# Late steps of a delta-rule recurrence: the largest block of products summed by TensorE through an identity matrix

## The chip, the cores and the metric

The kernel runs on one core of one Trainium2 chip. The metric is the device time of one execution in microseconds (us), here as the median of three runs. A core has TensorE (PE in the profile; its weight loads are PEld), VectorE (DVE), ScalarE (ACT), GpSimd (POOL) and SyncE (SP), which issues most of the DMAs. The engines run beside each other and wait for each other on semaphores.

## The reference

The layer works on 32 sequences of 32 tokens with 512 channels, in float32. It adds three parts to `x`, each after a layer norm: a cross attention to a context of 257 rows, a gated delta rule with 16 heads of 64, and a mixture of 8 experts with top 2 routing. The change lies in the delta rule, whose state is updated token by token:

```
def step(carry, x):
    S_f, S_s = carry
    ...
    S_f = fdt[..., None, None] * S_f
    S_s = sdt[..., None, None] * S_s
    err_f = vt - jnp.einsum('bhk,bhkv->bhv', kt, S_f)
    err_s = vt - jnp.einsum('bhk,bhkv->bhv', kt, S_s)
    bkt = bt[..., None, None] * kt[..., :, None]
    S_f = S_f + bkt * err_f[..., None, :]
    S_s = S_s + bkt * err_s[..., None, :]
    S_fc = _cap(S_f + rf * S_s)
    S_sc = _cap(S_s + rf * S_f)
    ot = fgt[..., None] * jnp.einsum('bhk,bhkv->bhv', qt, S_fc) + sgt[..., None] * jnp.einsum('bhk,bhkv->bhv', qt, S_sc)
```

`_cap` divides a state by max(1, its norm / 64). So each of the 32 steps needs the norm of the states of the step before it.

## The kernel before

The parts follow each other as blocks of code: layer norm, cross attention (`attend`), the projections and Gram matrices of the delta rule (`project`), the recurrence (`recurrence`, line 927), its outputs (`outputs`), routing, and the experts. Each block says what every engine does, in an order written out by hand; a semaphore that an engine waits for is met by a count.

The recurrence never forms the 64 x 64 states. It keeps, for each of the 512 pairs of sequence and head (128 partitions times `SG` = 4), coefficients over the tokens seen so far. `G` holds the Gram matrices of keys, queries and values, `psi` and `phi` are the coefficients of the two states (index `a`), `pr` is `psi` times a column of the key Gram matrix. The costly part of a step is a matrix times vector: for the next token `nxt`, `vp[i] = sum over j of G[i, j] * pr[j]` for the rows i up to `nxt`. There is a matrix of its own for each pair, so VectorE does it in two moves: it makes all the products (`products`, line 1065, into `prod`), and then sums them over j (`sums`, line 1072, a `tensor_reduce`). The matrix is symmetric up to a factor, and only its lower half is used: the rows are cut in blocks of `W` = 8, and the block of rows lo to hi has `min(lo + 8, nxt)` columns. A block has 2 * 4 * (hi - lo) * columns products in each partition, made in two halves (`a` = 0 and 1).

A step `t` on VectorE is written out as one list, with other work between dependent instructions: the reduction of the dots of the last step (line 1079), the products of block 0, `z` (1082), `zz` (1088), the products of the other blocks, the norms (1092, 1095), whose root ScalarE takes (1017), the sums of block 0, the cap (1103, 1106), the sums of the other blocks, the new coefficients `phi` (1114), and then the dots (1119), which read the whole of `vp`, the next `psi` (1041, 1042) and the next `pr` (1046), with which the next step begins. Beside that TensorE computes the gate projection of the layer in the first half of the recurrence (lines 1009, 1010, into all eight banks), ScalarE copies these results out from step 8 on (1021), and GpSimd makes the output weights (990 to 998). The products of a step are overwritten by those of the next.

Of the kernel before, what the change touches and what calls it, by code (L numbers as in the profile page):

```python
# [20 lines left out]
B, N, C = 32, 32, 512  # L21
TOK = B * N
NT = TOK // P
# [10 lines left out]
SG = B * H // P  # L34
BS = P // H
W = 8
# [29 lines left out]
class Chain:  # L66
# [8 lines left out]
    def mark(self, ins):  # L75

        self.n += 1
        ins.then_inc(self.sem, 1)
        return self.n

    def need(self, n):

        self.eng.wait_ge(self.sem, self.base + n)
# [840 lines left out]
                solve(SG - 1, range(N - 1, 0, -1))  # L924


def recurrence(nc, d, ps, xnT, G, gt, phi, wz, rf, gate, wg, wo_in):

    with ExitStack() as ctx:
        sb = lambda name, shape: ctx.enter_context(nc.sbuf_tensor(name, shape, F32))
        sem = lambda name: ctx.enter_context(nc.semaphore(name))
# [3 lines left out]
        prod = sb("r_prod", [P, PROD])  # L937
        z, zz, n2 = sb("r_z", [P, NZ, SG]), sb("r_zz", [P, SG, 3, NZ]), sb("r_n2", [P, 3, SG])
        pr, vp = [sb(f"r_pr{i}", [P, 2, SG, N]) for i in range(2)], sb("r_vp", [P, 2, SG, N])
# [6 lines left out]
        own, zeroed, psi_ready, out_done, stored = sem("r_own2"), sem("r_zeroed"), sem("r_psir"), sem("r_outd"), sem("r_stored")  # L946
        nm_ready, root_ready, blank_out = sem("r_nmr"), sem("r_rootr"), sem("r_blank_out")
        g_in, g_done, g_used, blocks_zero = sem("g_in"), sem("g_done"), sem("g_used"), sem("blocks_zero")
        POOL_STEPS = 4
        LATE = 8  # L950

        def bc(ap, shape):
            return ap.to_broadcast([P] + shape)

        with nc.Block() as block:
            @block.sync
            def _(sp):
                sp.dma_start(wg[:, :, :], d["Wg"].rearrange("(k p) n -> p k n", p=P)).then_inc(g_in, 16)
                for c in range(HC):
# [9 lines left out]
                             d["Wo"].rearrange("(c p) n -> p c n", p=P)).then_inc(wo_in, 16)  # L969
                sp.wait_ge(out_done, N * POOL_STEPS)  # L970
                for s in range(SG):
# [5 lines left out]
            def _(pool):  # L977
# [6 lines left out]
                for t in range(N):  # L984
                    u, m, n = t % PSI, t + 1, t * POOL_STEPS
                    if t == N - 3:
# [13 lines left out]
            @block.tensor  # L1000
            def _(pe):
                pe.wait_ge(g_in, 16 * (HC + 1))
                pe.wait_ge(zeroed, 3)
                for n in range(2 * NT):
                    t, hf = n // 2, n % 2
                    if n >= 8:
                        pe.wait_ge(g_used, n - 7)
                    for k in range(KC):
                        pe.matmul(ps[n % 8], xnT[:, k, t * P:(t + 1) * P], wg[:, k, hf * 512:(hf + 1) * 512], start=(k == 0), stop=False)  # L1009
                    pe.matmul(ps[n % 8], ones[:, :], bg[:, hf * 4:(hf + 1) * 4, :].rearrange("o c p -> o (c p)"),  # L1010
                              start=False, stop=True).then_inc(g_done, 1)

            @block.scalar
            def _(act):
                for t in range(N):
                    act.wait_ge(nm_ready, t + 1)
                    nc.scalar.activation(root[:, :, :], nm[:, :, :], ACT.Sqrt).then_inc(root_ready, 1)  # L1017
                    n = t - LATE
                    if 0 <= n < 2 * NT:
                        act.wait_ge(g_done, n + 1)  # L1020
                        nc.scalar.copy(gate[:, n // 2, (n % 2) * 8:(n % 2 + 1) * 8, :].rearrange("p h k -> p (h k)"), ps[n % 8]).then_inc(g_used, 1)
                act.wait_ge(g_used, 2 * NT)
                for t in range(NT):
                    rows = gate[:, t, :, :].rearrange("p h k -> p (h k)")
                    nc.scalar.activation(rows, rows, ACT.Silu)

            @block.vector
            def _(dve):
# [7 lines left out]
                def spread_states(t):  # L1036

                    u, m = t % PSI, t + 1
                    if t >= PSI:
                        dve.wait_ge(out_done, (t - PSI + 1) * POOL_STEPS)  # L1040
                    stt(psi[u][:, 0, :, 0:m], phi[:, 1, :, 0:m], rf1, phi[:, 0, :, 0:m], ALU.mult, ALU.add)
# [9 lines left out]
                for t in range(N):  # L1051
                    u, m, nxt = t % PSI, t + 1, t + 1
                    rows, parts, at = [], [], 0
                    if nxt < N:
                        need(pr_ready)
                        rows = [(x, min(x + W, nxt + 1), min(x + W, nxt)) for x in range(0, nxt + 1, W)]
                        for lo, hi, cols in rows:
                            size = 2 * SG * (hi - lo) * cols
                            parts.append(prod[:, at:at + size].rearrange("p (a s i j) -> p a s i j", a=2, s=SG, i=hi - lo))
                            at += size  # L1060

                    def products(x, a):
                        if x < len(rows):
                            lo, hi, cols = rows[x]
                            ins = tt(parts[x][:, a], G[:, :, lo:hi, 2, 0:cols], bc(pr[nxt % 2][:, a, :, None, 0:cols], [SG, hi - lo, cols]), ALU.mult)  # L1065
                            return mark(ins)

                    def sums(x):
                        if x < len(rows):
                            lo, hi, cols = rows[x]  # L1070
                            need(made[x])
                            return mark(red(vp[:, :, :, lo:hi].rearrange("p a s i -> p (a s) i"),
                                            parts[x].rearrange("p a s i j -> p (a s) i j"), AX.X, ALU.add))
                        return summed
# [8 lines left out]
                    else:  # L1083
                        products(0, 0)
                    made[0] = products(0, 1)
                    if z_ready is not None:
                        need(z_ready)
# [19 lines left out]
                    if nxt == N:  # L1107
# [7 lines left out]
                    pairs = mark(tt(sc[:, 2:6, :].rearrange("p (a b) s -> p a b s", a=2), bc(sc[:, 0:2, None, :], [2, 2, SG]),  # L1115
                                    bc(sc[:, None, 0:2, :], [2, 2, SG]), ALU.mult))
                    need(summed)
                    for a in range(2):
                        dots_ready = mark(tt(dots[:, a, :, :, 0:nxt], vp[:, :, :, 0:nxt], bc(pr[nxt % 2][:, a, None, :, 0:nxt], [2, SG, nxt]), ALU.mult))
                    need(phi_ready)  # L1120
# [176 lines left out]
def delta_rule(nc, d, ps, ident, x_nat, xnT, w_k, bias, wk_in):  # L1297

    with nc.sbuf_tensor("r_gram", [P, SG, N, 3, N], F32) as G, nc.sbuf_tensor("r_gates", [P, SG, NG + 1, N], F32) as gt, \
            nc.sbuf_tensor("r_phi", [P, 2, SG, N], F32) as phi, nc.sbuf_tensor("r_wz", [P, SG, N, 3, NZ], F32) as wz, \  # L1300
            nc.sbuf_tensor("r_rf", [P, 1], F32) as rf, nc.semaphore("wo_in") as wo_in:
        project(nc, d, ps, ident, xnT, G, gt, phi, wz, rf, w_k, bias, wk_in)
        with nc.sbuf_tensor("o_gate", [P, NT, H, DK], F32) as gate:
            recurrence(nc, d, ps, xnT, G, gt, phi, wz, rf, gate, w_k, wo_in)
            outputs(nc, d, ps, ident, x_nat, gate, w_k[:, :, :].rearrange("p k n -> p (k n)").rearrange("p (c n) -> p c n", c=HC), wo_in,
                    [xnT[:, 2 * s:2 * s + 2, :].rearrange("p k n -> p (k n)").rearrange("p (h n) -> p h n", h=H) for s in range(2)],
                    G[:, :, :, :, :].rearrange("p s i e n -> p (s i e n)"))
# [493 lines left out]
```

## Time and profile before

| | |
|---|---|
| median of 3 runs (lowest, highest) | 1950.63 us (1948.46, 1951.5) |
| the profiled execution | 1954.27 us |
| its span | 1952.5 us |
| VectorE busy over the span | 1192.9 us |
| TensorE busy over the span | 1586.1 us |
| recurrence, from the first row on line 1046 to the last on line 1106 | about 873 to 1126 us |

Busy times are those of an engine's own instructions. PEclk is the clock that TensorE was granted, as a share of 2.4 GHz, so 0.50 is 1.2 GHz. A float32 matmul appears as two matmul records (and two weight loads) in the trace, but a float32 transpose as one. Starts are in microseconds from the start of the span; an instruction's recorded time ends a little after the next one on its engine has begun, because they are pipelined.

### The profile page before, as it was taken

The page shows a single profiled execution, that of the slowest core. Times are in us where ns is not written, and L with a number is a line of the kernel's source. Part 1 is how long each engine was busy: PE and PEld are TensorE (multiplying, and loading weights), DVE is VectorE, ACT ScalarE, POOL GpSimd, SP SyncE. Part 2 cuts the span into 40 slices and gives each one's busy share as a digit, 9 for nine tenths or more (in the row PEclk, how much of TensorE's full clock was granted, in tenths as well). Part 3 has the DMA queues.
Part 4 walks back from the last instruction along what each step waited for, and adds up shares of the span by engine and source line. Part 5 has one row for each costly group of instructions (what it writes and reads, how often), then busy time and mean ns, then how long its engine had stood idle before and what let it go on. Part 6 is the DMA issues. An engine that isn't in the chain of part 4 may idle for free. (4 is left out here: it accounts for less than half of the span.)

```text
span 1952.5 us, 22186 instructions
## 1 busy us (share of the span) xinstructions
PE 1586.1 (81%) x7269; PEld 1151.5 (59%) x7269; DVE 1192.9 (61%) x2594; ACT 711.7 (36%) x1361; POOL 94.9 (5%) x261
## 2 busy tenths in 40 slices
PE   7999999999899999508700059749999999999998
PEld 3777777777677777403200048646666666666664
DVE  4355455465413677999999936344565555555555
ACT  2333333333244545400000032124555555555552
POOL 0000000000000000002111200030000000000003
PEclk9999999999899999858955559769999999999999
DMA  3211010010025145414100042064335515144104
GB/s 114 78 33 32 16 33 24 25 33 16 0 90 91 54 38 91 84 27 153 43 0 0 0 113 65 1 250 174 135 125 177 195 38 199 67 155 173 38 17 135
DMA packets 116457, 153.06 MB, mean 78 GB/s; under 512 B 47217, under 2 KB 68209, under 8 KB 116369
## 3 DMA queue, kind: packets, MB, share of 16 engines
q1 hardware_dynamic: 110640, 137.81, 23.7%
q0 software_dynamic: 2560, 8.39, 1.3%
q10 hardware_dynamic: 3168, 5.77, 0.8%
q8 instruction: 45, 0.74, 0.2%
q14 instruction: 44, 0.35, 0.1%
HBM read 250.32 MB, written 31.39 MB: 144 GB/s over the span
## 5 line engine op out<-in xcount | busy, mean ns | idle before, releaser
L1686 DVE TENSOR_TENSOR gl<-w_gu,gh 128x2048 fp32r<-128x2048 f32 x138 | 290.8, 2107 | 16.5 <-ACT gh L1621 16.5
L1621 ACT CAST gh<-w_gu 128x2048 fp32r<-128x2048 f32 x138 | 242.2, 1755 | 62.3 <-DMA w_gu<-in_up_proj 52.3
L1576 PE MATMUL bank<-w_d,hT 128*128 128x512 f32 x506 | 245.2, 603 | 13.6 <-ACT hT L1645 13.5
L1553 PE MATMUL bank<-gh,xh 128*128 128x512 f32 (+1 forms) x552 | 219.0, 397 | 10.9 <-DVE xl L1677 9.5
L1719 DVE TENSOR_TENSOR hid<-silu,bank 128x256 f32<-128x256 f32 x138 | 55.1, 399 | 262.9 <-ACT silu L1634 262.9
L1555 PE MATMUL bank<-gh,xl 128*128 128x512 f32 (+1 forms) x552 | 206.8, 375 | 0.0
L1554 PE MATMUL bank<-gl,xh 128*128 128x512 f32 (+1 forms) x552 | 206.6, 374 | 0.0
L1182 PE MATMUL bank<-o_v,xnT 128*128 128x64 f32 x256 | 36.1, 310 | 176.0 <-DMA o_v<-scratch_v_rows 176.0
L1576 PEld LDWEIGHTS bank<-w_d,hT 128*128 128x128 f32 x506 | 92.0, 189 | 88.4 <-issue 56.0
L1182 PEld LDWEIGHTS bank<-o_v,xnT 128*128 128x128 f32 x256 | 35.8, 227 | 176.8 <-DMA o_v<-scratch_v_rows 176.8
L1634 ACT ACTIVATE silu<-bank 128x256 f32<-128x256 f32 x138 | 50.7, 367 | 211.6 <-PE bank L1555 211.4
L550 DVE COPY probT<-bank 128x512 f32<-128x512 f32 x64 | 41.2, 683 | 138.5 <-PE bank L434 138.5
L1553 PEld LDWEIGHTS bank<-gh,xh 128*128 128x128 f32 x552 | 104.9, 190 | 32.3 <-DVE xl L1677 9.6
L1009 PE MATMUL bank<-w_kg,xnT 128*128 128x512 f32 x128 | 61.9, 629 | 75.1 <-DMA bg_row<-in_bg 75.1
L1555 PEld LDWEIGHTS bank<-gh,xl 128*128 128x128 f32 x552 | 104.6, 189 | 19.5
L1554 PEld LDWEIGHTS bank<-gl,xh 128*128 128x128 f32 x552 | 105.2, 191 | 14.7
L1017 ACT ACTIVATE r_root<-r_nm 128x8 f32<-128x8 f32 x32 | 6.7, 208 | 274.5 <-DVE r_nm L1095 274.5
L502 ACT ACTIVATE prob<-bank,neg_max 128x257 f32<-128x257 f32 x128 | 59.1, 474 | 86.9 <-DVE neg_max L537 86.9
L1009 PEld LDWEIGHTS bank<-w_kg,xnT 128*128 128x128 f32 x128 | 24.1, 198 | 111.3 <-DMA bg_row<-in_bg 75.3
L489 ACT COPY xv<-bank 128x512 f32<-128x512 f32 x64 | 37.6, 588 | 127.1 <-PE bank L387 127.1
L1065 DVE TENSOR_TENSOR r_prod<-r_gram,r_pr 128x512 f32<-128x512 f32 (+23 forms) x158 | 83.8, 549 | 0.0
L385 PE MATMUL bank<-xa_wkv_hi,ctx_hi 128*128 128x512 f32 x192 | 78.9, 411 | 0.6 <-PEq L280 0.6
(295 smaller groups left out, 3126.0 us busy)
## 6 DMA issues: line engine op xcount, KB each, us to landing
w_gu<-in_gate_proj SPq DMA_DIRECT2D x46, 1024.0 KB
w_gu<-in_up_proj SPq DMA_DIRECT2D x46, 1024.0 KB
w_d<-in_down_proj SPq DMA_DIRECT2D x46, 1024.0 KB
w_gu<-in_gate_proj SPq DMA_DIRECT2D x23, 768.0 KB
w_gu<-in_up_proj SPq DMA_DIRECT2D x23, 768.0 KB
w_d<-in_down_proj SPq DMA_DIRECT2D x23, 768.0 KB
ctx_raw<-in_ctxT SPq DMA_DIRECT2D x32, 385.5 KB, 3.9
scratch_gram<-gram SPq DMA_DIRECT2D x8, 768.0 KB, 3.3
```

What stands on the lines that cost most here:

```text
L385: pe.matmul(bank, hi(k), other_hi(k), start=(k == 0), stop=False)
L502: nc.scalar.activation(prob[s][:, c, :], ps[c][:, 0:M], ACT.Exp, bias=neg_max[s][:, c:c + 1], accum_out=total[s][:, c:c + 1]).then_inc(exp ...
L1009: pe.matmul(ps[n % 8], xnT[:, k, t * P:(t + 1) * P], wg[:, k, hf * 512:(hf + 1) * 512], start=(k == 0), stop=False)
L1065: ins = tt(parts[x][:, a], G[:, :, lo:hi, 2, 0:cols], bc(pr[nxt % 2][:, a, :, None, 0:cols], [SG, hi - lo, cols]), ALU.mult)
L1182: mm = pe.matmul(ps[O_BANK + 2 * s + h // 8][:, (h % 8) * DK:(h % 8 + 1) * DK], outw[s][:, h, :], v_row[s][:, h, :], start=True, stop=True)
L1553: pe.matmul(bank, xh[s % 2][:, k, :], hi, start=(k == 0), stop=False)
L1554: pe.matmul(bank, xh[s % 2][:, k, :], lo, start=False, stop=False)
L1555: mm = pe.matmul(bank, xl[s % 2][:, k, :], hi, start=False, stop=(k == KC - 1))
L1576: mm = pe.matmul(bank, hT[n % 2][:, c, :], w_d[:, b * (BLK // P) + c, :], start=(b == 0 and c == 0), stop=(b == NB - 1 and c == cs[-1]))
L1621: nc.scalar.copy(gh[n % RING][:, :, :, 0:bw].rearrange("p k a f -> p (k a) f"), w_gu[:, :, :, b * BLK:b * BLK + bw].rearrange("p k a f -> ...
L1686: nc.vector.tensor_tensor(gl[n % RING][:, :, :, 0:bw].rearrange("p k a f -> p (k a) f"), w_gu[:, :, :, b * BLK:b * BLK + bw].rearrange("p ...
L1719: nc.vector.tensor_tensor(hid[n % 2][:, 0:bw], silu[n % 2][:, 0:bw], ps[GU_BANK + n % 3][:, bw:2 * bw], ALU.mult).then_inc(hid_done, 1)
```

## The change

From `nxt` = `FIRST_SUM` = 18 on, that is in 14 of the 31 steps that have a matrix times vector, the block with the most products is taken first, and the others follow in their old order. Its products are made by VectorE as before. TensorE then sums them: for each column j it multiplies the 128 x 128 identity matrix (as the stationary operand) with the column's products, all `2 * SG * (hi - lo)` of them (64, or 56 in two steps), and adds up in bank 0. The columns' products lie `cols` elements apart. ScalarE copies the sums from the bank into `vp`, and VectorE waits for that copy ahead of the dots. The reduction of this block on VectorE is left out. The block has 16 columns for `nxt` = 18 to 21, 22 for 22, 23 for 23, 24 for 24 to 29, 30 for 30 and 31 for 31, so there are 314 such matmuls.

```
+        made_for_pe, pe_summed, vp_taken = sem("made_for_pe"), sem("pe_summed"), sem("vp_taken")
+        FIRST_SUM = 18
+        def row_blocks(nxt):
+            blocks = [(x, min(x + W, nxt + 1), min(x + W, nxt)) for x in range(0, nxt + 1, W)]
+            if nxt >= FIRST_SUM:
+                blocks.sort(key=lambda r: -(r[1] - r[0]) * r[2])
+                blocks[1:] = sorted(blocks[1:])
+            return blocks
...
@@ TensorE, behind the gate projection
+                pe.wait_ge(g_used, NT + 1)
+                for nxt in range(FIRST_SUM, N):
+                    k = nxt - FIRST_SUM
+                    lo, hi, cols = row_blocks(nxt)[0]
+                    width = 2 * SG * (hi - lo)
+                    part = prod[:, 0:width * cols].rearrange("p (x j) -> p x j", j=cols)
+                    pe.wait_ge(made_for_pe, 2 * (k + 1))
+                    if k:
+                        pe.wait_ge(vp_taken, k)
+                    for j in range(cols):
+                        mm = pe.matmul(ps[0][:, 0:width], ident[:, :], part[:, :, j], start=(j == 0), stop=(j == cols - 1))
+                    mm.then_inc(pe_summed, 1)
...
@@ ScalarE, step t, behind the root and the gate's copy
+                    k = t + 1 - FIRST_SUM
+                    if 0 <= k < N - FIRST_SUM:
+                        lo, hi, cols = row_blocks(t + 1)[0]
+                        act.wait_ge(pe_summed, k + 1)
+                        nc.scalar.copy(vp[:, :, :, lo:hi], ps[0][:, 0:2 * SG * (hi - lo)].rearrange("p (a s i) -> p a s i", a=2, s=SG)
+                                       ).then_inc(vp_taken, 1)
...
@@ VectorE, step t
-                        rows = [(x, min(x + W, nxt + 1), min(x + W, nxt)) for x in range(0, nxt + 1, W)]
+                        rows = row_blocks(nxt)
...
                             ins = tt(parts[x][:, a], G[:, :, lo:hi, 2, 0:cols], bc(pr[nxt % 2][:, a, :, None, 0:cols], [SG, hi - lo, cols]), ALU.mult)
+                            if x == 0 and nxt >= FIRST_SUM:
+                                ins.then_inc(made_for_pe, 1)
+                                return None
                             return mark(ins)
...
                     def sums(x):
-                        if x < len(rows):
+                        if x < len(rows) and not (x == 0 and nxt >= FIRST_SUM):
...
                     need(summed)
+                    if nxt >= FIRST_SUM:
+                        dve.wait_ge(vp_taken, nxt - FIRST_SUM + 1)
                     for a in range(2):
                         dots_ready = mark(tt(dots[:, a, :, :, 0:nxt], vp[:, :, :, 0:nxt], bc(pr[nxt % 2][:, a, None, :, 0:nxt], [2, SG, nxt]), ALU.mult))
```

VectorE, the step with `nxt` = 26, from the dots' reduction to the dots, as it stands before (`r_zr` is what comes of the dots, `r_prod` the products, `r_vp` their sums, and the last number is the elements in each partition):

```order
L1079 TENSOR_REDUCE r_zr<-r_dots 128x16
L1065 TENSOR_TENSOR r_prod<-r_gram,r_pr 128x256
L1082 TENSOR_TENSOR r_z<-r_zr,r_sc 128x16
L1065 TENSOR_TENSOR r_prod<-r_gram,r_pr 128x256
L1088 TENSOR_TENSOR r_zz<-r_wz,r_z 128x120
...
L1072 TENSOR_REDUCE r_vp<-r_prod 128x8x8
L1103 TENSOR_SCALAR r_root<-r_root 128x8
L1072 TENSOR_REDUCE r_vp<-r_prod 128x8x8
L1106 RECIPROCAL r_cap<-r_root 128x8
L1072 TENSOR_REDUCE r_vp<-r_prod 128x8x8
L1111 TENSOR_TENSOR r_sc<-r_cap,r_gates 128x8
L1072 TENSOR_REDUCE r_vp<-r_prod 128x8x3
```

And the same places of the same step in the change (line 1094 is the products, 1104 the sums):

```order
L1111 TENSOR_REDUCE r_zr<-r_dots 128x16
L1094 TENSOR_TENSOR r_prod<-r_gram,r_pr 128x768
L1114 TENSOR_TENSOR r_z<-r_zr,r_sc 128x16
L1094 TENSOR_TENSOR r_prod<-r_gram,r_pr 128x768
L1120 TENSOR_TENSOR r_zz<-r_wz,r_z 128x120
...
L1135 TENSOR_SCALAR r_root<-r_root 128x8
L1104 TENSOR_REDUCE r_vp<-r_prod 128x8x8
L1138 RECIPROCAL r_cap<-r_root 128x8
L1104 TENSOR_REDUCE r_vp<-r_prod 128x8x8
L1143 TENSOR_TENSOR r_sc<-r_cap,r_gates 128x8
L1104 TENSOR_REDUCE r_vp<-r_prod 128x8x3
```

The pair of products at the head of the step grew from 256 to 768 elements each, the pair of 768 later in the step is gone in exchange, and of four reductions three are left.

TensorE, behind the last gate matmul; the blocks for `nxt` = 18 to 21, then 22, 23 to 29, 30 and 31:

```order
L1021 MATMUL bank<-bg_row,ones_row 128x512
L1033 MATMUL bank<-r_prod,ident 128x64 x64
L1033 MATMUL bank<-r_prod,ident 128x56 x22
L1033 MATMUL bank<-r_prod,ident 128x64 x167
L1033 MATMUL bank<-r_prod,ident 128x56 x30
L1033 MATMUL bank<-r_prod,ident 128x64 x31
```

These 314 matmuls are new; before, TensorE had nothing here until the outputs.

## Rows read from the trace of the kernel before

**Rows 1.** The page, busy time of each engine over the span
```profile
PE 1586.1 (81%) x7269; PEld 1151.5 (59%) x7269; DVE 1192.9 (61%) x2594; ACT 711.7 (36%) x1361; POOL 94.9 (5%) x261
```
**Rows 2.** Windows: stretch, its length; busy us and instructions of PE, PEld, DVE, ACT, POOL; clock; DMA
```profile
1050.00:1070.00 20.00, 0.00 (x0) 0.00 (x0) 19.93 (x51) 0.21 (x1) 3.00 (x7) 0.50 0.00 0
```
**Rows 3.** Timeline of VectorE, the step with nxt = 26: start, time, instruction
```profile
1042.12 0.57 DVE L1079 TENSOR_REDUCE r_zr<-r_dots 128x16 f32<-128x400 f32 x1
1042.60 0.41 DVE L1065 TENSOR_TENSOR r_prod<-r_gram,r_pr 128x256 f32<-128x256 f32 x1
1043.02 0.42 DVE L1065 TENSOR_TENSOR r_prod<-r_gram,r_pr 128x256 f32<-128x256 f32 x1
...
1049.53 1.70 DVE L1072 TENSOR_REDUCE r_vp<-r_prod 128x64 f32<-128x1536 f32 x1
...
1052.55 0.65 DVE L1119 TENSOR_TENSOR r_dots<-r_vp,r_pr 128x208 f32<-128x208 f32 x2
...
1053.83 0.52 DVE L1046 TENSOR_TENSOR r_pr<-r_psi,r_gram 128x216 f32<-128x216 f32 x1
1054.38 0.59 DVE L1079 TENSOR_REDUCE r_zr<-r_dots 128x16 f32<-128x416 f32 x1
```
**Rows 4.** Groups of VectorE by shape, 955 to 1130 us: busy us, mean ns
```profile
L1065 DVE TENSOR_TENSOR r_prod<-r_gram,r_pr 128x512 f32<-128x512 f32 x30 | 20.5, 684 | 0.0
L1072 DVE TENSOR_REDUCE r_vp<-r_prod 128x64 f32<-128x1024 f32 x15 | 18.2, 1213 | 0.0
L1065 DVE TENSOR_TENSOR r_prod<-r_gram,r_pr 128x768 f32<-128x768 f32 x16 | 14.6, 952 | 0.0
L1072 DVE TENSOR_REDUCE r_vp<-r_prod 128x64 f32<-128x1536 f32 x8 | 13.6, 1701 | 0.0
...
L1065 DVE TENSOR_TENSOR r_prod<-r_gram,r_pr 128x992 f32<-128x992 f32 x2 | 2.3, 1183 | 0.0
...
L1072 DVE TENSOR_REDUCE r_vp<-r_prod 128x64 f32<-128x1984 f32 x1 | 2.2, 2209 | 0.0
```
**Rows 5.** Timeline of VectorE, starts of the first (nxt = 18) and behind the last step (31)
```profile
963.11 0.44 DVE L1079 TENSOR_REDUCE r_zr<-r_dots 128x16 f32<-128x272 f32 x1
...
969.55 0.67 DVE L1119 TENSOR_TENSOR r_dots<-r_vp,r_pr 128x144 f32<-128x144 f32 x2
...
971.34 0.45 DVE L1079 TENSOR_REDUCE r_zr<-r_dots 128x16 f32<-128x288 f32 x1
...
1123.27 0.66 DVE L1079 TENSOR_REDUCE r_zr<-r_dots 128x16 f32<-128x496 f32 x1
```
**Rows 6.** Timeline of the outputs behind the recurrence: matmuls, and ScalarE behind them
```profile
1140.46 7.09 PE L1182 MATMUL bank<-o_v,xnT 128*128 128x64 f32 x32 [175.98 <-DMA o_v<-scratch_v_rows]
...
1147.67 1.08 ACT L1225 ACTIVATE r_gram<-bank 128x512 f32<-128x512 f32 x2 [9.22 <-PE bank L1182]
...
1152.89 1.97 PE L1192 MATMUL bank<-ident,r_gram 128*128 128x128 f32 x8 [5.34 <-DVE r_gram L1289]
...
1154.65 6.92 PE L1182 MATMUL bank<-o_v,xnT 128*128 128x64 f32 x32
1161.34 0.77 PE L1206 MATMUL bank<-wo_hi,o_gT_hi 128*128 128x512 f32 x1
...
1169.64 3.68 PE L1182 MATMUL bank<-o_v,xnT 128*128 128x64 f32 x32
```
**Rows 7.** Windows, columns as in rows 2: behind the gate's matmuls, and in the outputs
```profile
964.00:966.00 2.00, 0.48 (x2) 0.00 (x0) 2.00 (x7) 0.00 (x0) 0.00 (x0) 1.00 0.03 4
966.00:968.00 2.00, 0.00 (x0) 0.00 (x0) 2.00 (x6) 0.68 (x2) 0.00 (x0) 0.85 0.88 274
...
1158.00:1160.00 2.00, 2.00 (x11) 2.00 (x11) 0.00 (x0) 0.00 (x0) 0.00 (x0) 0.50 0.00 0
1164.00:1166.00 2.00, 2.00 (x7) 1.58 (x6) 1.97 (x4) 0.31 (x1) 0.00 (x0) 0.66 0.90 235
```
**Rows 8.** Groups by shape: ScalarE's smallest copy out of a bank over 128 partitions
```profile
L293 ACT COPY k_last<-bank 128x128 f32<-128x128 f32 x1 | 0.3, 266 | 29.1 <-PE bank L312 29.1
```

More of the change, by code:

```diff
@@ L924, in _, with recurrence @@
                 solve(SG - 1, range(N - 1, 0, -1))
-def recurrence(nc, d, ps, xnT, G, gt, phi, wz, rf, gate, wg, wo_in):
+def recurrence(nc, d, ps, ident, xnT, G, gt, phi, wz, rf, gate, wg, wo_in):
     with ExitStack() as ctx:
@@ L1303, in delta_rule @@
         with nc.sbuf_tensor("o_gate", [P, NT, H, DK], F32) as gate:
-            recurrence(nc, d, ps, xnT, G, gt, phi, wz, rf, gate, w_k, wo_in)
+            recurrence(nc, d, ps, ident, xnT, G, gt, phi, wz, rf, gate, w_k, wo_in)
             outputs(nc, d, ps, ident, x_nat, gate, w_k[:, :, :].rearrange("p k n -> p (k n)").rearrange("p (c n) -> p c n", c=HC), wo_in,
```

## The prediction

> **What bounds the kernel now.** I read the page first, then windows of 20 us over the recurrence, then VectorE's timeline of single steps, and last the rows of TensorE that are nearest to the new matmuls. The page gives shares over the whole span and says little here: TensorE is the busier engine [rows 1], but not in the recurrence. In the window over its late steps VectorE is busy 19.93 of 20 us, while TensorE does nothing and its clock stands at 0.50, and ScalarE has 0.2 us of work [rows 2]. So in this stretch each microsecond that leaves VectorE's list is a microsecond gained, and each one that VectorE waits is one lost. The question is whether TensorE is done when VectorE comes to the dots.
>
> **What leaves VectorE.** The reductions taken away are that of 1024 elements four times (1.21 us each), that of 1536 six times (1.70), and one each of about 1.4, 1.6, 1.9 and 2.21 us; the first three of those four lie between the rows shown, in proportion to size [rows 4]. That is 4.9 + 10.2 + 7.1 = 22.2 us. Products are neither added nor removed. That their order changes costs nothing: what stood between dependent instructions was the products of a small block and is now that of a large one, so each gap is covered as before. The root is asked for before some 2.4 us of products, so ScalarE has it ready although the first reduction no longer stands ahead of line 1103. If nothing waited, the kernel would be 22 us faster.
>
> **What TensorE needs for one column.** The nearest rows are the head mixes of the outputs (line 1182): the same float32 form, 64 moving columns and a 128 x 128 stationary operand. 32 records, which are 16 matmuls, take 7.09 us from the first start to the last end, at a clock of 0.50 [rows 6]. One record lasts about 0.47 us, so their starts are (7.09 - 0.47) / 31 = 0.214 us apart, and a matmul of two records costs 0.427 us. At full clock the same 32 take 3.68 us, which makes 0.22 us a matmul. The transposes at the low clock, with 128 moving columns, are also (1.97 - 0.47) / 7 = 0.214 us apart [rows 6]. So what paces both is not the number of moving columns but the load of the weights, and the 56 columns of two steps will gain nothing. The identity is the same for every column, yet each matmul loads it: the page counts as many loads as matmuls [rows 1], although other places of the kernel use a stationary operand twice in a row.
>
> **Which clock.** 1.2 GHz, for these reasons. From 1152.89 to 1161.34 TensorE runs transposes and then such mixes for 8.4 us without a pause, and the window at 1158 to 1160 shows 0.50 still; so do the 7.09 us before. Only after the wide matmuls of 512 columns begin at 1161.34 does the clock rise, within the window 1164 to 1166 (mean 0.66) [rows 6, 7]. The new bursts look like the mixes, last 7 to 13 us, and stand apart by the rest of a step, some 4 us. A rule of the Trainium skill speaks the other way (TensorE: Matmul & The Clock Gate, Part 1 on the two states): sustained activity of TensorE releases the full clock, and idle time takes it back. The trace holds it for the wide matmuls and contradicts it for these narrow ones; what it would give here is a rival below. Only the first burst begins warm. The last gate matmul ends at 964.5, and the clock falls about 967.4 (mean 0.85 over 966 to 968) [rows 7]. With the first burst beginning at about 964.9, some 2.5 us of it run at double rate: -2.5 us.
>
> **The stride.** The 64 elements of a column are 64 to 124 bytes apart. No matmul of the trace reads so. VectorE does: line 1046 takes a strided column of the Gram matrix and needs 0.52 us for 216 elements, where line 1119 needs about 0.36 for each of its two instructions of 208 with neighbours side by side [rows 3]. Less 0.15 us that the smallest instructions take, that is 1.7 ns against 1.0 an element, a factor of 1.7. On TensorE 64 columns at 1.2 GHz are 53 ns, with this factor 90 ns, and 0.214 us pass in any case for the load. So I take nothing for the stride. The two bounds: nothing, and, if loads and streams did not overlap at all and the stride doubled the stream, 0.214 + 0.107 = 0.32 us a record, 0.64 us a matmul. I take the lower, since the equal spacing at 64 and 128 columns shows a stream hidden behind its load. The Trainium skill states against this change (SBUF — State Buffer, the note on cachelines) that float32 reads which touch a new 16-byte line each time pay a penalty; it gives no price, and by the rule alone the sum would lie anywhere up to the rival on the stride.
>
> **One step.** Take `nxt` = 26 [rows 3]. It lasts 1054.38 - 1042.12 = 12.26 us. In the change TensorE may start when both large products are done: the reduction on line 1079 (0.48 us to the next start), then twice 0.95 us [rows 4], 2.4 us after the step's start. Then come 24 x 0.427 = 10.25 us, and around them 0.69 us: the tail of the last record 0.26, VectorE to TensorE 0.06 and TensorE to ScalarE 0.12 (1147.55 to 1147.67) [rows 6], ScalarE's copy 0.22 (0.27 for 128 elements) [rows 8], and 0.03 to VectorE. Then VectorE has left what it does from the dots to the next step, 1.83 us. The path through TensorE is 2.4 + 10.25 + 0.69 + 1.83 = 15.2 us, VectorE's own list 12.26 - 1.70 + 0.08 = 10.6. So TensorE decides, and the step becomes 2.9 us longer, not 1.6 shorter; VectorE waits 4.6 us ahead of the dots. Queued behind that wait are psi, z and pr, so the whole next step; GpSimd and ScalarE only follow.
>
> **The sum.** The same in all steps: the first has 1.7 + 16 x 0.427 + 0.69 + 1.79 = 11.0 us in place of 8.23 [rows 5], and the TensorE path wins there too, by 4 us (the smallest lead, at `nxt` = 21, is 2.5 us). So the 14 steps can be added up as one path. From 963.11 to 1123.27 they take 160.2 us now [rows 5]. In the change: 314 matmuls x 0.427 = 134.1; the head's two products, 24.7 (4 x 1.37 + 6 x 1.90, and 7.8 in the other four, up to 2 x 1.18) [rows 4]; the reduction ahead of them 14 x 0.47 = 6.6; 14 x 0.69 = 9.7; from dots to the next step 24.7 (1.79 at first, 1.83 in the middle, 14 of them). That is 199.8 us, 39.6 more than now; with the warm start 37.1. What comes after is only shifted: the output's DMAs start when GpSimd is done, and the transfer of Wo hangs on the gate's matmuls alone. The profiled execution has 1952.5 us of span and 1.8 around it, 1954.3; the change would make it 1991.4. The median of the runs is 3.6 lower, so I forecast **1988 us**.
>
> **The rivals.**
> *The clock is full throughout* (1932 us, 5%). At 0.222 us a matmul the 24 columns take 5.3 us, with 0.65 around them, and VectorE has 6.3 us of other work there in the step above. Then VectorE's list decides in nearly all late steps, and 18.4 us of the 22.2 are gained. For it: the first burst starts warm. Against it: the clock falls within 3 us of an idle TensorE [rows 7], and a warm burst would leave about 4 us idle in each step.
> *The clock rises within each burst* (1952 us, 7%). This is what the skill's rule on the clock would make of it, and I price it by rows: as with the wide matmuls, 4.0 us at the low clock [rows 6, 7], the rest at the high one. The 24 columns then need 7.2 us in place of 10.25, the steps come out between 0.6 us shorter and 1 us longer than now, and the sum is +1.5 us. The 8.4 us at 0.50 speak against it.
> *The stride or the lack of overlap sets the pace* (2020 to 2055 us, 14%): 0.53 to 0.64 us a matmul instead of 0.427, which is 314 x (0.10 to 0.21) = 32 to 67 us on top of the forecast. For it: no row shows such a read on TensorE.
> *It does not do what it says*, say the reductions stay: excluded, since three of the four stand in the list of VectorE and 314 matmuls in that of TensorE.
>
> The point from which the sign turns is the price of a matmul: at 0.30 us the sum is nil, and each 0.01 us is worth 3 us. The forecast's 0.427 is well above it, the full clock's 0.22 below.
>
> **How the numbers follow.** The forecast has 72%; its own range is 1981 to 2000, from 0.41 to 0.46 us a matmul and 0.15 us either way in the 0.69. The strided rival has 14%, the clock within a burst 7%, the full clock 5%, others 2%. To hold 8 in 10 the range takes in the forecast and the lower part of the strided rival, and reaches down for a clock that is high part of the time: 1974 to 2040 us. A difference under 0.2%, or 3.9 us, cannot be told from none in this kernel. Faster: 6% (the full clock, and a little of the third case). Same: 6%. Slower: 88%.
>
> **What would show it.** In the profile of the changed kernel: 628 records on the new matmul's line, 0.214 us apart, at a clock of 0.50; in the timeline of VectorE an idle time ahead of the dots of 2.5 to 6 us in each of the 14 steps, 60 us in all, released by ScalarE's copy; a step with `nxt` = 26 of 15.2 us; a first burst shorter than the next three. The forecast is wrong if the window over the late steps shows a clock near 1.00, if starts are more than 0.22 us apart at the low clock (the stride), or if VectorE's idle time is small.

## The result

The changed kernel takes 1987.33 us (median of 4 runs, 1985.96 to 1988.35), the kernel before 1950.46 us beside it. The ratio is 1.018, with an interval of 1.017 to 1.020. The forecast was 1988 us.

The page after, busy time of each engine over the span; it answers to [rows 1]:

```profile
span 1985.0 us, 23470 instructions
...
PE 1720.2 (87%) x7897; PEld 1285.0 (65%) x7897; DVE 1172.5 (59%) x2580; ACT 714.8 (36%) x1375; POOL 95.3 (5%) x261
```

There are 628 records more on TensorE, two for each of the 314 matmuls, and VectorE has 20.4 us less to do. TensorE has 134.1 us more. The sum had 134.1 for its matmuls, but that the two agree to the tenth is chance: the new bursts shown below add up to 135.4 us, and the sum leads to 134.1 less 2.5 for the warm start plus 14 tails of 0.26, 135.2.

The timeline of VectorE over the first and behind the last of the 14 steps, to be held against [rows 5]:

```profile
964.61 0.44 DVE L1111 TENSOR_REDUCE r_zr<-r_dots 128x16 f32<-128x272 f32 x1
...
1161.30 0.66 DVE L1111 TENSOR_REDUCE r_zr<-r_dots 128x16 f32<-128x496 f32 x1
```

The stretch of the 14 steps grew from 160.16 to 196.69 us. These 36.5 us are the whole difference (1987.33 - 1950.46 = 36.9). Below, "the stretch" always means this one, from the first of these reductions to the last.

The step with `nxt` = 26, all engines, to be held against [rows 3]:

```profile
1064.05 0.57 DVE L1111 TENSOR_REDUCE r_zr<-r_dots 128x16 f32<-128x400 f32 x1
1064.53 0.95 DVE L1094 TENSOR_TENSOR r_prod<-r_gram,r_pr 128x768 f32<-128x768 f32 x1
...
1065.48 0.95 DVE L1094 TENSOR_TENSOR r_prod<-r_gram,r_pr 128x768 f32<-128x768 f32 x1
...
1077.05 0.21 ACT L1049 COPY r_vp<-bank 128x64 f32<-128x64 f32 x1 [9.15 <-PE bank L1033]
1077.36 0.66 DVE L1153 TENSOR_TENSOR r_dots<-r_vp,r_pr 128x208 f32<-128x208 f32 x2 [4.67 <-ACT r_vp L1049]
...
1079.20 0.59 DVE L1111 TENSOR_REDUCE r_zr<-r_dots 128x16 f32<-128x416 f32 x1
```

It lasts 15.15 us in place of 12.26. The bracket on the dots is VectorE's idle time, 4.67 us, ended by ScalarE's copy. Over the stretch, the view of who waited for whom (sum, times, longest):

```profile
DVE r_dots L1153 <- ACT r_vp L1049: 56.9, 14, 5.7
```

And TensorE's bursts, the first two, that of `nxt` = 26 and the last:

```profile
966.47 4.73 PE L1033 MATMUL bank<-r_prod,ident 128*128 128x64 f32 x32 [0.40 <-DVE r_prod L1094]
974.88 7.09 PE L1033 MATMUL bank<-r_prod,ident 128*128 128x64 f32 x32 [3.67 <-DVE r_prod L1094]
...
1066.49 10.52 PE L1033 MATMUL bank<-r_prod,ident 128*128 128x64 f32 x48 [4.60 <-DVE r_prod L1094]
...
1146.05 13.49 PE L1033 MATMUL bank<-r_prod,ident 128*128 128x64 f32 x62 [5.33 <-DVE r_prod L1094]
```

The 32 records of 16 columns take 7.09 us, exactly as long as the mixes of [rows 6]. The windows over the first burst and within the one of `nxt` = 26 and the last (columns as in rows 2):

```profile
966.00:968.00 2.00, 1.60 (x15) 1.56 (x14) 2.00 (x8) 0.42 (x2) 0.00 (x0) 1.00 0.24 56
968.00:970.00 2.00, 2.00 (x17) 2.00 (x15) 1.96 (x8) 0.26 (x1) 0.86 (x3) 0.76 0.90 282
...
1066.00:1076.00 10.00, 9.51 (x45) 9.51 (x45) 6.70 (x18) 0.21 (x1) 1.66 (x4) 0.50 0.00 0
1146.00:1159.00 13.00, 12.96 (x61) 12.96 (x61) 8.15 (x17) 0.21 (x1) 1.78 (x4) 0.50 0.00 1
```

TensorE is never idle for 13 us and the clock stays at 0.50. In the first burst it even falls, about 969, while the narrow matmuls run. That is 3 us after the last wide matmul of the gate, which ended at 966.1. In the kernel before the clock fell 2.9 us after it (964.5 to 967.4), with TensorE idle in between. As far as the clock shows, the narrow matmuls made no difference to it.

### The profile page after: what moved, and what is told of

Its sections match the earlier page's. It is cut to its first block and busy times, and to the rows that moved or that the text cites. A ratio compares the mean times of both kernels' runs of the same rounds, so it can differ in the third digit from the quotient of the medians.

```text
span 1985.0 us, 23470 instructions
## 1 busy us (share of the span) xinstructions
PE 1720.2 (87%) x7897; PEld 1285.0 (65%) x7897; DVE 1172.5 (59%) x2580; ACT 714.8 (36%) x1375; POOL 95.3 (5%) x261
## 5 line engine op out<-in xcount | busy, mean ns | idle before, releaser
L1720 DVE TENSOR_TENSOR gl<-w_gu,gh 128x2048 fp32r<-128x2048 f32 x138 | 290.8, 2108 | 16.3 <-ACT gh L1655 16.3
L1033 PE MATMUL bank<-r_prod,ident 128*128 128x64 f32 (+1 forms) x628 | 135.4, 404 | 58.1 <-DVE r_prod L1094 58.1
L1033 PEld LDWEIGHTS bank<-r_prod,ident 128*128 128x128 f32 x628 | 132.7, 327 | 61.4 <-DVE r_prod L1094 60.2
L1094 DVE TENSOR_TENSOR r_prod<-r_gram,r_pr 128x256 f32<-128x256 f32 (+21 forms) x158 | 83.8, 549 | 0.0
L1597 PEld LDWEIGHTS bank<-ident,hid 128*128 128x128 f32 x253 | 35.3, 140 | 67.3 <-issue 49.5
```

Of the source, the lines that this page charges most:

```text
L1033: mm = pe.matmul(ps[0][:, 0:width], ident[:, :], part[:, :, j], start=(j == 0), stop=(j == cols - 1))
L1597: mm = pe.transpose(ps[H_BANK + n % 2][:, c * P:(c + 1) * P], hid[n % 2][:, c * P:(c + 1) * P], ident[:, :])
L1720: nc.vector.tensor_tensor(gl[n % RING][:, :, :, 0:bw].rearrange("p k a f -> p (k a) f"), w_gu[:, :, :, b * BLK:b * BLK + bw].rearrange("p ...
```

## The experiments

The theory: TensorE's time for the block, paced by records of 0.214 us at the low clock, lies between the products and the dots, and VectorE waits for it. The rivals are VectorE's own list in its new order, contention, a fixed cost of the hand-over, the stride, and the clock.

**Order alone.** The new order of the blocks, with all sums left on VectorE:

```
-                        rows = [(x, min(x + W, nxt + 1), min(x + W, nxt)) for x in range(0, nxt + 1, W)]
+                        rows = row_blocks(nxt)
```

> The kernel before with the blocks in the new order (largest first from nxt = 18 on), all of them still summed by VectorE, no matmuls and no copies. Theory (the order costs nothing, each gap between dependent instructions is covered as before): 1950.5 us, within 0.2% of before. Rival (part of the loss is VectorE's own list in the new order): up to 0.5 us a step, 1957 us.

Measured: 1952.50 us against 1951.78, ratio 1.0005 (0.9996 to 1.0015). The stretch is 160.23 us, 0.07 longer than before. The order costs nothing.

**TensorE beside VectorE, and nobody late.**

```
-                    for j in range(cols):
+                    for j in range(cols // 2):
...
-                        nc.scalar.copy(vp[:, :, :, lo:hi], ps[0]
+                        nc.scalar.copy(aside[:, :, :, lo:hi], ps[0]
...
-                        if x < len(rows) and not (x == 0 and nxt >= FIRST_SUM):
+                        if x < len(rows):
```

> The changed kernel, but VectorE sums every block itself as before, and TensorE sums half of the largest block's columns (8 to 15) into the bank; ScalarE copies this half sum into a tile that nobody reads; VectorE keeps its wait for the copy ahead of the dots. Theory (the whole loss is the wait, and TensorE at work beside VectorE costs VectorE nothing): TensorE needs 8 x 0.427 + 0.69 = 4.1 us to 15 x 0.427 + 0.69 = 7.1 us and VectorE has 4.8 to 10 us of work there, so the copy is always in time: 1950.5 us within 0.2%, no idle time of VectorE ahead of the dots. Rival (contention for the memory, or the semaphores and the copy, cost something in themselves): 0.3 us or more a step, 1955 us or more.

Measured: 1953.62 us, ratio 1.0013 (1.0004 to 1.0023). The stretch is 160.27 us, and the trace has no wait ahead of the dots. So half the matmuls, all the copies and all the semaphores of the change cost 0.1 us where VectorE does not wait for them. The median is 1.8 us longer, but the profiled execution, 1951.88 us, is not one of the longer ones, so its trace cannot say where these 1.8 us lie; their cause stays open. Half of the columns is also half of the time beside VectorE. For the full bursts the changed kernel's own rows speak: the products of 256 elements that run beside a burst take 0.42 us there and 0.41 or 0.42 before. The loss of the change is the wait.

**Neighbours side by side.**

```
-                        mm = pe.matmul(ps[0][:, 0:width], ident[:, :], part[:, :, j], ...)
+                        mm = pe.matmul(ps[0][:, 0:width], ident[:, :], prod[:, j * width:(j + 1) * width], ...)
```

> The changed kernel, but each matmul reads 64 (56) neighbouring elements of the products instead of a column with its elements 64 to 124 bytes apart. Other products are added up than the computation asks for; number, size and order of the instructions are the same. Theory (the weight load paces the matmuls): starts stay 0.214 us apart, 7.09 us for the 32 records of 16 columns, time 1987 us within 3. Rival (the stride costs something): records closer together and a time below 1980 us, in proportion.

Measured: 1982.59 us in one run. Its burst of `nxt` = 26:

```profile
1064.78 10.51 PE L1033 MATMUL bank<-r_prod,ident 128*128 128x64 f32 x48 [4.59 <-DVE r_prod L1094]
```

10.51 us against 10.52: at the low clock the stride costs nothing. The stretch is 196.6 us, the changed kernel's 196.7. The 4 to 5 us by which this single run is shorter do not come from there, so I read the trace and not the total.

**Half the width.**

```
+                        mm = pe.matmul(ps[0][:, 0:width // 2], ident[:, :], part[:, 0:width // 2, j], ...)
```

> The changed kernel, but each matmul takes only half of the rows of the block (32 or 28 moving columns in place of 64 or 56); the sums of the other half are left out. Theory (the load of the 128 x 128 stationary operand paces): nothing changes, 0.214 us from record to record, 1987 us within 3. Rival (TensorE's time goes with the elements it sums): the wait ahead of the dots falls by 3.4 to 6.6 us a step, some 60 us of TensorE time less, and the time comes down to 1935 us or less.

Measured: 1986.13 us in one run.

```profile
1065.61 10.45 PE L1033 MATMUL bank<-r_prod,ident 128*128 128x32 f32 x48 [4.60 <-DVE r_prod L1094]
```

With 32 moving columns in place of 64 the same 48 records take 10.45 us. What is paid for is not the summed elements but the records, each with its load of the identity. That it is the load, and not some other fixed price of a record, no run separates. The loads of the kernel before, with 4, 16, 32, 80 and 128 stationary columns, all in stretches at full clock but for a few records, speak for it:

```profile
L430 PEld LDWEIGHTS bank<-ident,prob 128*4 128x4 f32 x32 | 2.7, 86 | 0.4
L706 PEld LDWEIGHTS bank<-q_sq,head_cols 128*16 128x16 f32 x64 | 3.9, 94 | 10.4 <-issue 9.4
L308 PEld LDWEIGHTS bank<-xa_wkv,ctx_last 128*32 128x32 f32 x6 | 0.6, 109 | 2.0 <-issue 2.0
L723 PEld LDWEIGHTS bank<-xnT,w_gates 128*80 128x80 f32 x32 | 4.5, 149 | 3.3 <-issue 1.7
L303 PEld LDWEIGHTS bank<-xnT,xa_wq 128*128 128x128 f32 x64 | 12.1, 190 | 16.0 <-issue 15.7 <-DVE qT L321 0.2
```

From 16 to 128 columns a load grows by 96 ns, 0.86 ns a column. For 128 columns that is 0.11 us, an estimate from these rows, and the narrow records of the first, warm burst start 0.11 us apart.

**One record a column.**

```
+        prod_r = ctx.enter_context(nc.sbuf_tensor("r_prod_r", [P, 2 * SG * W * (N - 1)], F32R))
+        ident_r = ctx.enter_context(nc.sbuf_tensor("r_ident_r", [P, P], F32R))
...
-                        mm = pe.matmul(ps[0][:, 0:width], ident[:, :], part[:, :, j], ...)
+                        mm = pe.matmul(ps[0][:, 0:width], ident_r[:, :], part[:, :, j], ...)
```

> The changed kernel, but the products of the largest block and the identity are kept as fp32r, so that a column is one matmul record (and one weight load) and not two; the products are rounded to fp32r. Theory (records of 0.214 us at a clock of 0.50 pace TensorE): a column costs 0.214 us, 24 columns 5.1 us, which is less than VectorE's other work from nxt = 25 on, and the kernel comes out like the rival of the full clock, 1932 us, between 1929 and 1937. Rival (a fixed cost of the hand-over from VectorE to TensorE to ScalarE and back makes a good part of the loss): the waits fall by less than half, 1955 us or more.

Measured: 1934.58 us, ratio 0.991 (0.989 to 0.993). The burst of `nxt` = 26, and the waits for the copy over the stretch:

```profile
1041.18 5.33 PE L1037 MATMUL bank<-r_prod_r,r_ident_r 128*128 128x64 f32 x24 [4.77 <-DVE r_prod_r L1102]
```

```profile
DVE r_dots L1161 <- ACT r_vp L1054: 0.7, 2, 0.4
```

24 records instead of 48, half the time, still at 0.50 of the clock, and the wait is gone: 0.7 us in all. The stretch is 139.95 us. The same change of the kernel loses 1.8% with two records a column and gains 0.9% with one. The fixed part of the hand-over does not make the loss: it is the same here, and the wait is gone.

**A warm TensorE.** Wide matmuls behind each burst:

```
+                    for _ in range(5):
+                        pe.matmul(ps[1], ident[:, :], G[:, 0, :, :, :].rearrange("p i e n -> p (i e n)")[:, 0:512], start=True, stop=True)
```

> The changed kernel with five wide matmuls (512 moving columns of the Gram matrix, into a bank that nobody reads) behind each burst of narrow ones, so that TensorE is busy while VectorE makes the next products. Theory (wide matmuls raise the clock after about 4 us, narrow ones do not hold it): from the second or third step on a burst begins at a clock of 1.00 and falls to 0.50 some 2.5 us later, as the first burst of the changed kernel did; the 24 columns take about 8 us in place of 10.5, and the time is 1960 us, between 1952 and 1970. Rivals: the clock, once high, is held through the burst, 1935 us; or it never rises, and the wide matmuls, which last 4.3 us at the low clock, only push the early bursts back, 1988 us or more.

Measured: 1971.03 us in one run, just past the end of what I gave. TensorE's timeline in the third step and in that of `nxt` = 24 (line 1034 the narrow ones, 1039 the wide), and then windows over the latter:

```profile
985.45 3.71 PE L1034 MATMUL bank<-r_prod,ident 128*128 128x64 f32 x32
988.99 4.49 PE L1039 MATMUL bank<-r_gram,ident 128*128 128x512 f32 x10
...
1027.08 9.06 PE L1034 MATMUL bank<-r_prod,ident 128*128 128x64 f32 x48
1035.95 7.04 PE L1039 MATMUL bank<-r_gram,ident 128*128 128x512 f32 x10
```

```profile
1027.00:1029.00 2.00, 2.00 (x14) 1.92 (x13) 2.00 (x8) 0.68 (x2) 0.00 (x0) 1.00 0.00 0
1029.00:1031.00 2.00, 2.00 (x14) 2.00 (x14) 2.00 (x5) 0.00 (x0) 1.10 (x3) 0.96 0.00 0
1031.00:1033.00 2.00, 2.00 (x12) 2.00 (x11) 0.79 (x4) 0.00 (x0) 0.44 (x1) 0.50 0.00 0
...
1037.00:1039.00 2.00, 2.00 (x4) 0.89 (x3) 1.97 (x9) 0.00 (x0) 0.00 (x0) 0.50 0.00 0
1039.00:1041.00 2.00, 2.00 (x3) 0.67 (x2) 2.00 (x5) 0.00 (x0) 0.00 (x0) 0.50 0.02 4
1041.00:1043.00 2.00, 2.00 (x7) 0.93 (x6) 2.00 (x7) 0.21 (x1) 0.00 (x0) 0.98 0.00 0
```

The clock rises and falls much as expected, and the time is neither rival's. In the steps with 16 columns a burst is over in 3.7 us, at full clock. The burst of `nxt` = 30 keeps it too, for 6.8 us. In the other long ones the clock falls while they run, in the step shown about 4 us after the narrow matmuls begin (at 1031), though TensorE is never idle, and comes back about 5 us after the wide ones begin (at 1041). The wide ones then last 7.04 us at the low clock and hold back the next burst, which is one reason why it came out 11 us above the 1960.

The other reason is in the same trace. At full clock the narrow records are not 0.11 us apart in every step. Here are a window within the burst of `nxt` = 25, with 24 columns, and the burst of `nxt` = 30, with 30, and a window within it:

```profile
1043.00:1047.00 4.00, 4.00 (x27) 4.00 (x27) 3.65 (x11) 0.00 (x0) 1.67 (x4) 1.00 0.03 6
```

```profile
1115.92 6.83 PE L1034 MATMUL bank<-r_prod,ident 128*128 128x56 f32 x60
```

```profile
1116.00:1122.00 6.00, 6.00 (x56) 6.00 (x55) 6.00 (x14) 0.21 (x1) 1.24 (x3) 1.00 0.00 0
```

The starts of single records are 0.160 us apart with 24 columns, and 0.111 with 16 or 30. The elements of a column lie 96 bytes apart with 24 columns, 64 with 16 and 120 with 30. So the distance may well cost something at the full clock that the 0.214 us of the low clock cover. No run has neighbours side by side in such a burst at full clock, so this is not shown. The bursts of 24 columns took 8.6 to 9.1 us and not the 8 that I had expected. Worked out from these rows, the step with `nxt` = 26 would last 12.6 us at full clock throughout (2.4 + 24 x 0.32 + 0.65 + 1.83), no less than the 12.26 before. That is an estimate. The clock is worth much here, but in these steps it would not have turned the sign, and wide matmuls that compute nothing are a poor way to it.

**Four columns a matmul.** Four partial sums a row stay in the bank, and VectorE sums them itself in place of ScalarE's copy:

```
+                        for j in range(0, cols, PER):
+                            some = min(PER, cols - j)
+                            mm = pe.matmul(bank[:, :, lo - low:hi - low, 0:some], ident[:, :], part[:, :, :, j:j + some], ...)
...
+                        dve.wait_ge(pe_summed, nxt - FIRST_SUM + 1)
+                        red(vp[:, :, :, low:high].rearrange("p a s i -> p (a s) i"),
+                            ps[0][:, 0:2 * SG * (high - low) * PER].rearrange("p (x i j) -> p x i j", x=2 * SG, j=PER), AX.X, ALU.add).then_inc(vp_taken, 1)
```

> The changed kernel, but one matmul takes four columns at once (256 moving elements, 224 in two steps) and adds them into 256 elements of the bank, where four partial sums a row are left; VectorE sums these four out of the bank ahead of the dots, in place of ScalarE's copy. Theory (up to 256 moving columns hide behind the load): still 0.214 us a record, so 4 to 8 matmuls of 0.427 us a step, 1.7 to 3.4 us; no wait is left; VectorE saves 22.2 us of reductions and pays 14 x 0.42 us: 1934 us, between 1931 and 1938. Rival (a matmul costs in proportion to its moving columns at 256, or reads from the bank are slow): 1945 us or more.

Measured: 1937.48 us, ratio 0.993 (0.991 to 0.995). No wait is left, the stretch is 144.98 us, and the last reduction takes 0.41 us on average. But the time agrees with the theory only because VectorE no longer waits. The burst of 8 records at the low clock (`nxt` = 19):

```profile
973.35 3.75 PE L1040 MATMUL bank<-r_prod,ident 128*128 128x256 f32 x8 [5.47 <-DVE r_prod L1096]
```

A record with 256 columns costs 0.427 us from start to start at this clock, not 0.214. That part of the theory fell.

**Four columns, side by side.**

```
+                            mm = pe.matmul(ps[0][:, 0:n * some], ident[:, :], prod[:, j * n:(j + some) * n], ...)
```

> The kernel with four columns a matmul, whose records turned out 0.44 us apart at a clock of 0.50 and not 0.214; here each matmul reads 256 (224) neighbouring elements, so other products are added up. Theory (a float32 stream takes two cycles a column, so that 256 columns are 512 cycles and outlast the 256 cycles of the load): records as far apart as before, the bursts of 8 records at the low clock still 3.75 us, time about 1937 us. Rival (the stride of the runs of four halves the rate): 0.214 us a record, bursts of 2.1 us; the time stays the same in either case, since VectorE does not wait there.

Measured: 1942.16 us in one run. The same burst:

```profile
974.76 3.75 PE L1041 MATMUL bank<-r_prod,ident 128*128 128x256 f32 x8 [3.98 <-DVE r_prod L1096]
```

3.75 us again, and the stretch is 145.5 us, as good as the 145.0 with the stride; the rest of the single run's 1942.16 lies elsewhere. So it is not the stride either at this width and clock: 0.427 us for 256 columns are two cycles a column at 1.2 GHz. At that rate 128 columns take 0.214 us, as long as the load; the next experiment has that case.

**Two columns a matmul.** `PER` = 2 in place of 4.

> As the kernel with four columns a matmul, but with two (128 moving elements), so that VectorE has two partial sums a row left. Theory (load and stream take 256 cycles each): 0.427 us a matmul at the low clock, 5.1 us for 24 columns, the same TensorE time as with four; VectorE's last reduction is 0.14 us shorter, but in the first six steps TensorE is up to 0.8 us late, 3 us in all: 1937 us, between 1933 and 1941. Rival (the weight load cannot be hidden behind a stream of its own length): 0.6 us a matmul, waits in all steps and 1950 us or more.

Measured: 1935.69 us, ratio 0.992 (0.990 to 0.995), the stretch 143.66 us, waits 0.3 us in all. Load and stream of equal length hide each other: 16 records take 3.75 us in the steps where 8 records with 256 columns took 3.75. The stretch is 1.3 us shorter than with four columns, since the last reduction takes 14 times 0.28 us and not 0.41; the medians of the two, 1935.69 and 1937.48 us, are too close to be told apart.

**Two blocks in float32.** The two largest blocks, four columns a matmul, into one bank.

```
+        PER, BLOCKS = 4, 2
...
-                blocks[1:] = sorted(blocks[1:])
+                blocks[BLOCKS:] = sorted(blocks[BLOCKS:])
```

> As the kernel with four columns a matmul, but the two largest blocks go to TensorE, one behind the other into one bank, and VectorE sums what is left of both with one reduction of up to 512 elements. Theory: VectorE saves 30 us in all, TensorE needs 2.6 to 6.0 us a step and is done before VectorE comes to it or within 0.3 us: 1921 us, between 1918 and 1927. Rival (the second block's products come too late, so TensorE is on the path again): waits of 1 us or more a step and 1934 us or more, no better than with one block.

Measured: 1953.61 us, ratio 1.0009 (0.9998 to 1.0020). The wait and the time are those of the rival:

```profile
DVE r_vp L1156 <- PE bank L1040: 23.7, 14, 2.8
```

But the rival's reason, products that come too late, does not hold. The burst of `nxt` = 25 and the products of the second block beside it:

```profile
1041.60 6.24 PE L1040 MATMUL bank<-r_prod,ident 128*128 128x256 f32 x20 [5.11 <-DVE r_prod L1096]
```

```profile
1042.44 0.69 DVE L1096 TENSOR_TENSOR r_prod<-r_gram,r_pr 128x512 f32<-128x512 f32 x1
```

These products are ready at 1043.13, 1.5 us after the burst began, and the 12 records of the first block keep TensorE busy for longer than that. What failed is the price of a matmul. I had reckoned 10 matmuls of 0.427 us for `nxt` = 26; they cost twice that at the low clock, as the experiments above show, and the burst took 7.4 us with the clock high for a part of it. Everything that VectorE's list lost came back as a wait: the stretch is 161.8 us.

**Two blocks, one record.** The same two blocks in fp32r, two columns a matmul (`PER, BLOCKS = 2, 2`).

> The two largest blocks on TensorE with products and identity in fp32r (products rounded to that type), two columns a matmul, VectorE sums the two partial sums a row of both blocks with one reduction of up to 256 elements. Theory (a record of up to 128 columns costs 0.214 us at the low clock): 12 to 30 records a step, 2.6 to 6.4 us, done before VectorE comes to them; VectorE saves 39 us of reductions and pays 14 x 0.4: 1917 us, between 1912 and 1923. Rival (as with two blocks in float32, the second block's sums come too late): waits of 1 us or more a step, 1930 us or more.

Measured: 1929.95 us against 1954.45, ratio 0.988 (0.986 to 0.990). The stretch is 136.1 us, 24 shorter than before; I had expected 34. The waits are 1.9 us in all:

```profile
L1158 DVE TENSOR_TENSOR r_sc<-r_cap,r_gates 128x8 f32<-128x8 f32 x14 | 6.0, 429 | 0.0
...
L1169 DVE TENSOR_REDUCE r_vp<-bank 128x128 f32<-128x256 f32 (+4 forms) x14 | 5.6, 397 | 1.9 <-PE bank L1046 1.9
```

The reductions fell from 56.0 us of busy time to 16.3 and 5.6. Some of the rest is in the rows: each removed reduction overlapped its neighbour by 0.09 us (28 of them, 2.5 us), and the small operation on line 1158 takes 429 ns where it took 260 before (2.4 us). It lies beside GpSimd's work, which starts behind the cap; that this is the cause is a reading of the trace, and no run tests it. The last few us I did not take apart; gaps between dependent instructions that the removed reductions had covered are a guess.

The fp32r versions round the products of these blocks, and what that does to the recurrence's accuracy was not studied. In full float32 two columns a matmul are 0.8% faster than the kernel before, and four are 0.7%.

## Why the prediction was right

*What bounds the stretch.* Right. Time came only from VectorE's list and its waits; order, contention and copies cost 0.1 us of the stretch at most.

*What leaves VectorE.* 22.2 us reckoned, 20.4 in the busy times. A reduction overlaps the next instruction by 0.08 us, which 14 times is 1.2 of the 1.8 missing.

*What TensorE needs.* 0.427 us a matmul reckoned, (10.52 - 0.47) / 47 x 2 = 0.428 measured. That records pace it is now shown from two sides: half the moving columns leave the time as it is, half the records, in another type, halve it. That it is their load rests on the rows of loads above. One step of the argument was lucky. I read the transposes' equal spacing at 128 columns as a load that hides its stream. But a stream of 128 columns lasts as long itself, and the loads of the transposes are shorter than those of the mixes, 221 against 332 ns in the kernel before, both at 0.50:

```profile
L1192 PEld LDWEIGHTS bank<-ident,r_gram 128*128 128x128 f32 x8 | 1.6, 221 | 5.5 <-DVE r_gram L1289 5.5
L1182 PEld LDWEIGHTS bank<-o_v,xnT 128*128 128x128 f32 x3 | 0.8, 332 | 0.0
```

So the transposes may well go at the pace of their stream, and the equal 0.214 us was no evidence for the load. For 64 columns that made no difference; for the kernel with two blocks it decided the sign.

*The clock.* Right: 0.50 in 13 of 14 bursts, up to 13.5 us long, and a warm beginning of the first. That burst was 2.4 us shorter than the next (4.73 against 7.09), where 2.5 were taken. The rival of a full clock, though, was priced too low: it took 0.222 us a matmul for every step, and at full clock the steps with 24 columns show 0.32. By the estimate above, its 1932 us would not have come even with the full clock. The Trainium skill's rule on activity (TensorE: Matmul & The Clock Gate, Part 1) does not hold as it stands for these narrow matmuls: issued without a pause, they neither raised the clock nor held it.

*The stride.* Right to take at nothing at the low clock, where it costs no time: 10.52 against 10.51 us with 64 columns, 3.75 against 3.75 with 256. The Trainium skill warns of a penalty for each new 16-byte line (SBUF — State Buffer, the note on cachelines). None is seen in these two pairs; the 0.160 us a record at full clock with 24 columns may be one, and that stays open.

*The sum.* 15.2 us for `nxt` = 26 and 15.15 measured, 37.1 us in all and 36.5 measured. Around the matmuls of this step there are 0.62 us (1066.49 to 1077.36 less 24 x 0.427) where 0.69 were taken; 14 times that is 1.0 us. The waits were to be 60 us and are 56.9, of which the warm first burst explains 2.4.

## What to carry to other kernels

Work that leaves the busiest engine helps only if the helper is done before the result is needed: reckon for the single step the path through the helper against the work left beside it, not the busy shares. For narrow matmuls count records and weight loads, and give each load as many moving columns as it hides; here two columns of 64 a matmul turned a loss of 1.8% into a gain of 0.8%. Do not take the price of a record beyond the widths that a row shows: 64 and 128 columns cost the same, 256 twice as much. Take the rate from a row of the same form at the clock that such work gets, since a narrow burst may never see the high clock.

## What the runs showed of the hardware

- Narrow float32 matmuls (64 columns, a load each) keep TensorE busy without a gap, yet its clock falls from 1.00 to 0.50 while they run, 2.5 us after the first burst began and 3.6 us after the wide matmuls ended in the step with `nxt` = 24 of the warm experiment. With 256 columns a matmul, and a TensorE that was busy about half of the time, the clock did rise, toward the end of a burst or behind it, so most of its high time fell on gaps. A window of that kernel over a burst and the gap behind it, and the end of that burst:

```profile
1050.00:1060.00 10.00, 4.49 (x12) 3.22 (x11) 9.93 (x29) 0.21 (x1) 1.68 (x4) 0.67 0.00 0
1053.00:1054.40 1.40, 1.40 (x5) 0.88 (x4) 1.40 (x4) 0.00 (x0) 0.52 (x2) 0.74 0.00 0
```

- Records of 128 columns, 0.213 us apart in both kernels, raised the clock in float32 and not in fp32r. Windows over the same stretch of the kernel with two columns a matmul, and of that with two blocks in fp32r:

```profile
1030.00:1040.00 10.00, 5.02 (x24) 4.79 (x24) 9.93 (x29) 0.21 (x1) 1.58 (x4) 0.67 0.00 1
```

```profile
1030.00:1040.00 10.00, 4.64 (x23) 4.48 (x22) 9.93 (x29) 0.21 (x1) 1.67 (x4) 0.50 0.00 1
```

- At 1.2 GHz a float32 record cost 0.21 us with 32, 64 or 128 moving columns and 0.427 with 256. That is the longer of its load and two cycles a moving column.
- At full clock the same narrow records were 0.111 us apart in the steps with 16 or 30 columns and 0.160 in those with 24, in the warm experiment.
